# State-space layer on one core: segment sums from two tiles of 64 rows, and the causal convolution as four shifted products

## What the layer computes

```
zxbcdt = h @ in_proj_w.T                 # z 256, xBC 512, dt 32 columns; h = layernorm(x)
xBC    = silu(causal_conv(xBC, conv_w, conv_b))   # 4 taps per channel, over the 128 tokens
dt     = sigmoid(dt + dt_bias) * 0.099 + 0.001    # as the kernel computes it
cum    = cumsum(dt * -exp(A_log))        # per head, 32 heads, over the tokens
L[h]   = exp(cum[t] - cum[s]) for s <= t # the segment sums, a 128x128 matrix for each head
y      = (L * (C B^T)) @ (x * dt) + D_skip * x
out    = norm(y * silu(z)) @ out_proj_w.T
```

## Time and profile before

| | |
|---|---|
| runs | 3611.14, 3614.72, 3620.63 us, median 3614.72 |
| profiled execution | 3598.95 us, its span 3597.2 us |
| TensorE busy in the span | 2647.8 us (74%) |
| VectorE | 2113.8 us (59%) |
| ScalarE | 1368.2 us (38%) |
| GpSimd | 572.8 us (16%) |
| mean granted TensorE clock | 0.857 |
| first and last `mix` of the layer start at | 66.4 and 489.8 us |

### The profile page before, as it was taken

The page is one execution under the profiler, slowest core; times in us unless marked ns, Lnnn a source line. Parts: engine busy times, 40 slices in busy tenths (PEclk is TensorE's granted clock), DMA queues, the critical chain, the costliest instruction groups (busy, mean ns, idle before and its releaser), DMA issues. The chain is left out here.

```text
span 3597.2 us, 53583 instructions
## 1 busy us (share of the span) xinstructions
PE 2647.8 (74%) x20619; PEld 1585.3 (44%) x20644; DVE 2113.8 (59%) x4142; ACT 1368.2 (38%) x2371; POOL 572.8 (16%) x581
## 2 busy tenths in 40 slices
PE   4777768999969969996886999558879962443351
PEld 2454445666654424443443444435554540222251
DVE  4887853444447735544664543457773225999756
ACT  3555424555533212221332443238762321444321
POOL 1223320000000003332331000011113011000003
PEclk8888868999979979997997999769988985776675
DMA  2000000000000010000000000200010011000010
GB/s 79 1 2 1 1 7 4 4 7 4 4 1 1 1 61 2 2 2 10 10 8 1 1 1 0 78 21 7 11 29 27 28 39 30 1 1 1 17 53 24
DMA packets 40514, 51.98 MB, mean 14 GB/s; under 512 B 8843, under 2 KB 30420, under 8 KB 39124
## 3 DMA queue, kind: packets, MB, share of 16 engines
q1 hardware_dynamic: 38228, 44.45, 3.8%
q0 software_dynamic: 2048, 4.20, 0.4%
HBM read 39.45 MB, written 9.18 MB: 14 GB/s over the span
## 5 line engine op out<-in xcount | busy, mean ns | idle before, releaser
L135 POOL TENSOR_TENSOR l_rstd<-l_moments,w-1_minus_half 128x4 f32<-128x4 f32 x104 | 114.2, 1098 | 1599.2 <-DVE l_moments L129 1599.0
L1211 DVE TENSOR_REDUCE l_top<-l_p_score 128x4 f32<-128x1024 f32 x64 | 78.4, 1225 | 223.3 <-PE l_p_score L997 223.3
L1416 PE MATMUL l_p_gate<-l_h_t,w_wg 128*128 128x512 f32 x400 | 208.4, 603 | 0.4 <-issue 0.4
L1439 PE MATMUL l_p_out<-l_hidden,w_wd 128*128 128x512 f32 x400 | 204.4, 594 | 4.2 <-DVE l_hidden L1709 2.9
L2909 DVE SCALAR_TENSOR_TENSOR l_mix<-l_decay,l_cb 128x1024 f32<-128x1024 f32 x128 | 163.7, 1288 | 60.3 <-ACT l_decay L2810 55.3
L814 DVE TENSOR_REDUCE l_top<-l_ring 128x8 f32<-128x1024 f32 x128 | 150.7, 1220 | 69.3 <-PE l_ring L630 69.0
L348 ACT ACTIVATE l_probs<-l_probs,l_minus_top 128x128 f32<-128x128 f32 x512 | 156.8, 393 | 53.4 <-DVE l_minus_top L418 53.4
L1709 DVE TENSOR_TENSOR l_hidden<-l_act_out,l_p_spread 128x512 f32<-128x512 f32 x128 | 85.7, 685 | 128.9 <-ACT l_act_out L1537 128.7
L2810 ACT ACTIVATE l_decay<-l_p_seg 128x1024 f32<-128x1024 f32 x128 | 129.4, 1022 | 75.2 <-PE l_p_seg L2664 75.0
L3184 PE MATMUL l_p_s<-w-1_ident,l_z 128*128 128x128 f32 x128 | 26.9, 399 | 178.1 <-ACT l_z L3223 178.1
L141 DVE TENSOR_SCALAR l_h<-x_res,l_moments,l_rstd 128x128 f32<-128x128 f32 (+1 forms) x384 | 113.7, 358 | 48.9 <-POOL l_rstd L135 48.6
(11 more groups left out here) (486 smaller groups left out, 6384.0 us busy)
## 6 DMA issues: line engine op xcount, KB each, us to landing
l_c_t<-in_ctx_t SPq DMA_DIRECT2D x24, 256.0 KB, 2.7
l_rows_in<-l_zero SPq DMA_DIRECT2D x1, 2432.0 KB
l_tile_h<-l_rows_in SPq DMA_DIRECT2D x38, 64.0 KB, 1.9
l_rows_out<-l_tile_y SPq DMA_DIRECT2D x38, 64.0 KB, 1.5
x_res<-in_x SPq DMA_DIRECT2D x1, 2048.0 KB, 7.5
w_mask<-in_mask SPq DMA_DIRECT2D x1, 2048.0 KB, 9.1
w_wg<-in_l2f_wg SPq DMA_DIRECT2D x1, 2048.0 KB
w_wu<-in_l2f_wu SPq DMA_DIRECT2D x1, 2048.0 KB
```

Source lines behind the costliest of these rows:

```text
L135: return nc.gpsimd.tensor_tensor(rstd[:, :], moments[:, :, 1], minus_half[:, 0:moments.shape[1]], ALU.pow)
L1416: nc.tensor.matmul(p_gate[k % 2][:, :], w["wg"][:, s, :], h_t[:, g % 4, :], start=True, stop=True)\
L1439: nc.tensor.matmul(p_out[:, :], w["wd"][:, s, :], hidden[:, k % 4, :], start=(s == 0), stop=(gated and s == steps - 1)).then_inc(down, 1)
```

## The change

It has two parts. First, the 32 heads are laid out in two tiles of 64 rows, the even heads in one and the odd ones in the other, each with three parts of 16 rows and 16 rows for the mask. The matmuls of the segment sums then have 64 rows, and those of the two tiles alternate, each tile into its own bank. The split uses a column `less` of factors, so that one instruction serves all 128 partitions. Second, the convolution moves into the projection: `conv_in_of` holds the projection's weights times each tap's weight (built once), `h_t` has three zero columns ahead of each sequence, and each block of 128 channels is four matmuls over shifted windows of `h_t`, accumulated in PSUM. The taps on VectorE and the padded copy on ScalarE are gone. The four blocks are now at n = 3, 4, 5 and 6, `time_steps` and `time_bias` at n = 6, and `time_step` at n = 8. `conv_w` becomes a broadcast load of 8 KB for each partition, and two small tables (`steps`, `less`) are loaded more.

```diff
-                    nc.tensor.matmul((p_b, p_a)[c % 2][:, :], w["conv_in"][:, c * T:(c + 1) * T], h_t[:, :],
-                                     start=True, stop=True).then_inc(conv_in, 1)
+                    for k in range(TAPS):
+                        last = nc.tensor.matmul((p_b, p_a)[c % 2][:, :], conv_in_of[:, k, c * T:(c + 1) * T],
+                                                h_t[:, :, k:k + T], start=(k == 0), stop=(k == TAPS - 1))
+                    last.then_inc(conv_in, 1)
...
-                    for half in range(2):
-
-                        first = part * QH + 4 * half
-                        out = p_seg[n % 2][:, half, :]
-                        nc.tensor.matmul(out, parts[0:3 * NH, q, u * T:(u + 1) * T],
-                                         bcast(minus[:, first:first + 4], [3 * NH, 4, T], 2), start=True, stop=False)
-                        for k in range(4):
-                            last = nc.tensor.matmul(out[:, k * T:(k + 1) * T], pick[:, first + k, :],
-                                                    parts[:, q, u * T:(u + 1) * T], start=False, stop=(k == 3))
+                    tile = lambda odd: slice(odd * TILE, (odd + 1) * TILE)
+                    for odd in range(2):
+                        nc.tensor.matmul(p_seg[n % 2][:, odd, :], parts[tile(odd), q, u * T:(u + 1) * T],
+                                         bcast(minus[tile(odd), 4 * part:4 * part + 4], [TILE, 4, T], 2), start=True, stop=False)
+                    for k in range(4):
+                        for odd in range(2):
+                            last = nc.tensor.matmul(p_seg[n % 2][:, odd, k * T:(k + 1) * T], pick[tile(odd), 4 * part + k, :],
+                                                    parts[tile(odd), q, u * T:(u + 1) * T], start=False, stop=(k == 3))
                     last.then_inc(seg_done, 1)
...
-                            if n == 3:
-                                project(j, 0)
-                                project(j, 1)
-                            if n == 4:
-                                project(j, 2)
-                                project(j, 3)
-                            if n == 5:
+                            if n in (3, 4, 5, 6):
+                                project(j, n - 3)
+                            if n == 6:
                                 time_steps(j)
...
-                    nc.scalar.copy(padded[:, c, :, TAPS - 1:], source)
-                    nc.scalar.activation(conv[:, q, c, :, :], source, ACT.Identity, bias=w["conv_b"][:, c:c + 1],
-                                         scale=w["conv_w"][:, c, TAPS - 1:TAPS]).then_inc(padded_ready, 1)
+                    nc.scalar.activation(conv[:, q, c, :, :], source, ACT.Identity, bias=w["conv_b"][:, c:c + 1])\
+                        .then_inc(conv_biased, 1)
...
-                    split_high(nc, p_b, high, parts[0:3 * NH, q, :]).then_inc(high_ready, 1)
+                    nc.scalar.copy(high[:, :], p_b[:, :]).then_inc(high_ready, 1)
...
-                nc.vector.tensor_copy(pick[0:3 * NH, :, :], bcast(w["head_row"][:, :], [3 * NH, NH, T], 2))
-                nc.vector.tensor_copy(pick[3 * NH:, :, :], bcast(w["blocks"][3 * NH:, 0, :], [T - 3 * NH, NH, T], 1))
-                nc.vector.tensor_copy(parts[3 * NH:, :, :].rearrange("p q (u t) -> p (q u) t", t=T),
-                                      bcast(w["blocks"][3 * NH:, 1, :], [T - 3 * NH, 2 * GROUP, T], 1))
+                nc.vector.tensor_tensor(pick[:, :, :], bcast(w["head_row"][:, :], [T, NH // 2, T], 2),
+                                        bcast(w["blocks"][:, :], [T, NH // 2, T], 1), ALU.add)
...
-                nc.vector.memset(padded[:, :, :, :].rearrange("p c u t -> p (c u t)"), 0.0)
+                nc.vector.memset(h_t[:, :, 0:TAPS - 1], 0.0)
+                nc.vector.tensor_tensor(conv_in_of[:, :, :], bcast(w["conv_in"][:, :], [D, TAPS, NC * T], 1),
+                                        w["conv_w"][:, :].rearrange("p (k c) -> p k c", k=TAPS), ALU.mult)
...
-                    for c in (2 * pair, 2 * pair + 1):
-                        last = nc.vector.scalar_tensor_tensor(conv[:, q, c, :, :], padded[:, c, :, k:k + T],
-                                                              w["conv_w"][:, c, k:k + 1], conv[:, q, c, :, :],
-                                                              ALU.mult, ALU.add)
...
+                    order.then(nc.vector.scalar_tensor_tensor(rest[:, :], high[:, :], w["less"][:, 0:1], p_b[:, :],
+                                                              ALU.mult, ALU.add))
+                    order.then(nc.vector.tensor_copy(middle[:, :], rest[:, :]))
+                    nc.vector.scalar_tensor_tensor(parts[:, q, :], middle[:, :], w["less"][:, 1:2], rest[:, :],
+                                                   ALU.mult, ALU.add).then_inc(parts_ready, 1)
...
-                        if n in (5, 6, 7):
-                            tap(j, q, 0, n - 5)
-                        if n == 5:
+                        if n == 6:
                             time_bias(j)
-                        if n == 7:
+                        if n == 8:
                             time_step(j, q)
-                        if n in (8, 9, 10):
-                            tap(j, q, 1, n - 8)
```

105 lines of the change are left out of this document (48 added, 57 removed).

## The result

| | before | changed |
|---|---|---|
| median of six runs each, us | 3616.94 | 3637.90 |
| lowest and highest, us | 3611.14, 3623.61 | 3632.28, 3640.42 |
| profiled execution, its span, us | 3598.95, 3597.2 | 3637.33, 3635.4 |
| first and last `mix` of the layer start at, us | 66.4, 489.8 | 68.5, 507.0 |

The ratio is 1.0052, with a 95% interval of 1.0038 to 1.0066: slower by 0.5%, or 21 us between the medians. The profiled executions lie further apart, 38 us. In the state-space layer the last `mix` starts 17.2 us later; the last part of the layer behind it is as long in both, within 0.3 us. So the other 21 us of that pair arise behind the layer, where nothing was changed: they are a difference between two executions.

A forecast was written before the change was run, and what follows sets the result against it. TensorE and VectorE alternate in setting a group's time, ScalarE its end. 14.4 + 3 + 1 - 1.5 + 1.5 = 18.4 us on 3598.95 gives 3617.4, on the median's scale 3633; range 3625 to 3643.

The forecast's parts named there:

- Rival C: Whole kernel: VectorE's gain counts in full, TensorE's delay does not, by cheaper shifted matmuls or slack; faster, 3567 without delay; chance 0.12.
- Segments: TensorE's segment-sum matmuls: pairs on two 64-row tiles overlap, so `segments` takes 0.54 us instead of 0.98.
- rival A: TensorE's `segments`: the small matmuls don't overlap and keep 0.98 us; +32 us, 3647; chance 0.15.
- TensorE's chain: TensorE from `h_t` to `output`: a step with a block takes 4.8 us, `output` starts at 20.0 instead of 10.8.
- The waits on VectorE: VectorE from `time_bias` to the square of step 12: waits for TensorE, less taps, put the square at 35.9 instead of 33.5.
- GpSimd's price: VectorE's `mix` 10, `mix` 11 and `gated` beside GpSimd's `add_output`: slowed by 1.9 us a group in all.
- B's and the last: Two signs of being wrong: `mix` 10 and 11 at 1.2; square to `decay` 14 other than 7.1.
- Rival B: VectorE beside GpSimd: `mix` 10, 11 and `gated` take plain times; +0.5 a group, +5 us, 3620; chance 0.20 with the like.
- Groups: Six groups with a previous group's output: each 2.4 us longer, 58.7 us, 14.4 in all.
- the term for more of it: TensorE's clock in the groups: less work ahead of the blocks, so more of the lower clock, 1.5 us in all.
- First group: First group, with no `output` to wait for: TensorE 9.2 us late, less taps, no slack from mean squares; +3 us.
- Start and last group: Start: shorter setup, 12 more matmuls, 12 taps gone, +1.0 us; last group: VectorE's 1.23 replaces TensorE's 1.55, about -1.5.

The follow-up runs named there:

- the run with two of four taps: Changed kernel with only the last two of the four shifted matmuls of each convolution block; ratio to the kernel before 0.9887.
- its own experiment: Changed kernel with GpSimd's three instructions of `add_output` cut to two columns; ratio to the kernel before 1.0023.
- the sigmoid's move: Changed kernel with the sigmoid of the time steps back at step 7, ahead of the mean squares; ratio to the kernel before 1.0015.
- the early output: TensorE's `output` of the previous group moved from step 7 to 3; ratios to before: 1.0054 on changed kernel, 1.0024 on tiles alone, 1.0028 on before.

## Why the prediction was right

The forecast was +18.4 us or 0.51%, the measurement is 0.52%, and the layer's own part 17.2 us. Its steps, in their order:

**Convolution on TensorE.** 3.6 us a block, 3.64 measured. Rival C wanted a matmul 0.22 us cheaper; it is not, so C fell with that row, and its other half, a delay that slack takes up, with the run with two of four taps.

**Segments.** 0.54 us, 0.54 measured, so rival A fell: eight matmuls of 128 columns with eight loads, and the change to the column tiles, take 0.32 us (311.87 to 312.19). The load price of the Trainium skill (TensorE: Matmul & The Clock Gate, section on LDWEIGHTS) would give an estimate of 0.85 us for eight in a queue; no such queue shows in this row.

**TensorE's chain.** `output` at 20.0, measured 19.81. A step of 4.8, measured 4.75. The change of shape at 0.1 us held: eight passes at 0.43 us are 3.44, and a block with a change on either side is 3.64; it is all that the drain told of in the Trainium skill, TensorEngine Tiling, section Tiling Modes, costs here.

**The waits on VectorE.** After `h_t`: bias 19.2 forecast and 18.8 measured, `mix` 8 22.2 and 21.97, `mix` 9 28.6 and 28.95, `mix` 10 31.0 and 31.1, `mix` 11 32.9 and 32.8, square 35.9 and 35.97. The first two are right by their reasons. Behind them three errors cancel, and that is luck. A wait of 0.61 us for the output's product ahead of the gate was not foreseen; it made `mix` 9 late. GpSimd's price was taken as 1.9 us and is 0.9 in these rows (`mix` 11 0.49 over its 1.22, the gate's product 0.44 over its 0.42), of which at most 0.7 arrives by its own experiment; `mix` 10 took the plain 1.22 us in all six groups. And `mix` 11 waited 0.49 us for `decay` 11, since `running_sums` ran at the lower clock (1.67 us). So the walk was right to 0.1 us, and its last terms were not. In the two groups of 58.1 us `mix` 11 is plain as well and the square comes at 34.9, with 7.5 us from there to `decay` 14: both signs that the prediction had named for being wrong, B's and the last, are there in two groups of six. Rival B was right about `mix` 10 in all groups and about `mix` 11 in two, about the gate's product in none, and still not about the time. Its own sum slipped, too: 18.4 less six times 1.9 is 7 us, not 5.

**Groups.** 2.4 us longer forecast for six of them, 14.4 in all, and 1.5 for the clock. Measured: 353.3 us (123.4 to 476.7) for 340.4 before, +12.9 with the clock's share in it. The lower clock cost before 1.5 us in group 1 and the changed kernel 1.9 us in its group 5, so the term for more of it was wrong: it changed places and added 0.4. Without it six groups are 12.5 us longer, 2.1 each. The 2.4 hold for the groups like the one read closely. In it VectorE is busy 36.5 us and TensorE 46.1, near the 35 and 45 that were forecast.

**First group.** +3 forecast, +5.2 measured (54.9 for 49.7). This term was mis-sized. The clock fell at `running_sums`, behind a wait of 2.80 us for VectorE, and `mix` 11 then waited 1.93 us. From the square to `decay` 14 it is 8.2 us there, 7.1 before, as `decay` 13, which stands ahead of the silus, waited 0.99 us for its segments:

```profile
102.66 2.08 PE L2608 MATMUL l_p_b<-w_upto,l_da 128*128 128x128 f32 x8 [2.80 <-DVE l_da L2855]
```

```profile
106.81 1.23 DVE L2887 SCALAR_TENSOR_TENSOR l_mix<-l_decay,l_cb 128x1024 f32<-128x1024 f32 x1 [1.93 <-ACT l_decay L2793]
```

**Start and last group.** Start +1.0 forecast, +2.1 measured. The setup came out as costed:

```profile
24.99 2.29 DVE L2818 TENSOR_TENSOR l_pick<-w_head_row,w_blocks 128x2048 bf16<-128x2048 f32 x1
...
30.15 0.18 DVE L2830 TENSOR_SCALAR l_neg_a<-l_neg_a 128x32 f32<-128x32 f32 x1
```

It ends at 30.33 instead of 33.57, 3.2 us earlier (2.9 forecast; the broadcast of `conv_w` cost nothing). From there it is 5.3 us longer where 3.9 were counted: the bias comes 7.7 us later after the first block (17.05 for 9.35), and 2.4 come back behind it, where three of the six pairs of taps stood. Last group: its `mix` instructions take 30.3 us from the first to the last, 33.3 before, -3.0 for -1.5.

The terms then: 12.9 + 5.2 + 2.1 - 3.0 = 17.2, against 14.4 + 1.5 + 3 + 1 - 1.5 = 18.4. The large term is right by its mechanism, which the run with two of four taps, the sigmoid's move and the run of the convolution alone each bear out; the others missed by 1 to 2 us each with opposite signs, so that the sum comes within 1.2 us is luck in part.

## What to carry to other kernels

Where engines alternate in setting the time, ask of each piece of work in which part it stands, not how busy its engine is. Freeing 9.5 us on the engine with the larger busy time lost 2 us a group here, as the work went to the engine that sets another part of the group. Moving VectorE's taps one step earlier, so that one pair fell into a wait and none ran long beside GpSimd, was worth 2.3 us a group in the kernel before and 3.6 with the tiles (lower clocks included). And move work into a wait only without what feeds it: the early output brought its TensorE half into TensorE's own busy stretch and gained nothing even where the clock was full.

## What the runs showed of the hardware that was not expected

The granted clock of TensorE fell while it was busy without a gap: 1.00 over the mean squares (sixteen matmuls of 2 columns), 0.52 over the product behind them, 0.97 over the block after it. The product's sixteen matmuls took 3.4 us for 1.8 to 2.0. It happened behind mean squares at 1.00 in several groups of several kernels, not in all, and matmuls added ahead of `h_t` did not prevent it. What decides it was not tried.

Beside GpSimd's instructions of 512 elements a pair of taps took 3.42 us for 1.41 in one place and 1.41 in another, where GpSimd's multiplication took 4.64 for 1.26 instead. `mix` 11 took 1.22, 1.71 or 2.29 us from group to group of one kernel, and in the two groups with 1.22 GpSimd's multiplication took 3.32 us, in the others 2.18. So the price moves from one engine to the other with small shifts in time, and a term read from one place does not carry over to another.
